# A hybrid convolution and attention kernel on Trainium2: the first attention's pairs of images written out in every engine's program in place of a loop

## What is computed

```python
x = (input - mean) * scale + shift
qkv = einsum('oc,bchw->bohw', pw_w, x)                 # 4 heads of 32 channels
attn = softmax(einsum('bnchw,bncyx->bnhwyx', q, k) / sqrt(32), over the last axis x)
out = einsum('bnhwyx,bncyx->bnchw', attn, v); x = out_w @ out + out_b + input
# then, on the 1024 tokens of each image:
t = t + attention(layernorm(t))     # 64 heads of 2 channels, causal in blocks of 512, rmsnorm on q and k
t = t + experts(layernorm(t))       # 8 experts, three 128x128 products each, gated by a softmax
```

## Time and profile before

| | us |
|---|---|
| median of 3 runs | 3389.75 |
| the three runs | 3385.29 to 3397.03 |
| profiled execution, its own time | 3398.41 |
| profiled execution, span from first to last instruction | 3396.7 |
| PE busy | 3078.5 (91%) |
| ACT busy | 2711.0 (80%) |
| DVE busy | 2062.5 (61%) |
| POOL busy | 263.9 (8%) |

### The profile page before, as it was taken

The page is one execution under the profiler, slowest core; times in us unless marked ns, Lnnn a source line. Parts: engine busy times, 40 slices in busy tenths (PEclk is TensorE's granted clock), DMA queues, the critical chain, the costliest instruction groups (busy, mean ns, idle before and its releaser), DMA issues.

```text
span 3396.7 us, 70341 instructions
## 1 busy us (share of the span) xinstructions
PE 3078.5 (91%) x27633; PEld 1087.3 (32%) x27633; DVE 2062.5 (61%) x2974; ACT 2711.0 (80%) x2580; POOL 263.9 (8%) x350
## 2 busy tenths in 40 slices
PE   6899999999798898998999899899998988999999
PEld 3444444444322222222222222222222222233444
DVE  4788878888656456556556556656656643443333
ACT  5444444445499999999999999999999999973555
POOL 6000000000110011011010110101101000000000
PEclk9899999999899999999999999999999999998999
DMA  6121211120100110210210210210210211001000
GB/s 224 53 53 44 53 47 34 44 52 20 53 16 18 59 26 18 61 27 17 59 29 18 59 27 20 59 27 17 60 29 18 59 27 37 19 15 63 13 12 12
DMA packets 132542, 135.73 MB, mean 40 GB/s; under 512 B 27414, under 2 KB 111476, under 8 KB 132220
## 3 DMA queue, kind: packets, MB, share of 16 engines
q1 hardware_dynamic: 131216, 130.44, 13.9%
q10 hardware_dynamic: 1004, 0.83, 0.1%
HBM read 70.31 MB, written 51.41 MB: 36 GB/s over the span
## 4 chain that ended last, share of the span: by engine, by line
ACT 39%; PE 35%; issue 19%; DVE 5%; DMA 1%; SPq 1%; ACTq 0%; POOL 0%; DVEq 0%
ACT arena L961 38%; PE ps L1318 5%; PE ps L1371 3%; PE ps L1040 3%; PE ps L1365 3%; PE ps L1087 3%; PE ps L1406 3%; PE ps L1114 3%; PE ps L1089 3%; PE ps L1098 2%; PE ps L1069 2%; PE ps L1270 2%; DVE arena L1480 1%; DVE arena L1487 1%; DVE arena L1492 1%
## 5 line engine op out<-in xcount | busy, mean ns | idle before, releaser
L961 ACT ACTIVATE arena<-ps 128x1536 f32<-128x1536 f32 x1536 | 2068.3, 1636 | 21.6 <-PE ps L1270 21.2
L1318 PE MATMUL ps<-arena 128*32 128x512 f32 (+3 forms) x12288 | 1257.8, 504 | 1.9 <-DVE arena L1755 1.7
L1755 DVE TENSOR_TENSOR arena<-arena,causal 128x512 f32<-128x512 f32 x1024 | 664.5, 688 | 314.1 <-ACT arena L961 304.6
L1270 PE MATMUL ps<-arena 15*128 15x512 bf16 (+3 forms) x6144 | 606.9, 331 | 160.7 <-ACT arena L961 151.1
L890 ACT ACTIVATE arena<-ps 128x512 f32<-128x512 f32 x512 | 299.8, 596 | 278.8 <-PE ps L1089 268.2
L1270 PEld LDWEIGHTS ps<-arena 15*128 15x128 bf16 x6144 | 163.0, 92 | 1100.6 <-ACT arena L961 958.7
L1318 PEld LDWEIGHTS ps<-arena 128*32 128x32 f32 x12288 | 284.7, 109 | 385.1 <-issue 331.4
L1480 DVE TENSOR_REDUCE arena<-ps 128x32 bf16<-128x1024 f32 x256 | 311.2, 1216 | 119.9 <-PE ps L1069 119.9
L1487 DVE TENSOR_TENSOR arena<-arena,ps 128x512 f32<-128x512 f32 x512 | 329.2, 680 | 33.5 <-PE ps L1098 32.6
L1740 DVE COPY arena<-ps 128x512 f32<-128x512 f32 x256 | 176.5, 690 | 219.9 <-PE ps L1318 218.9
L1087 PE MATMUL ps<-arena 96*128 96x256 bf16 x1024 | 260.7, 279 | 0.3 <-ACT arena L863 0.2
(11 more groups left out here) (200 smaller groups left out, 1970.9 us busy)
## 6 DMA issues: line engine op xcount, KB each, us to landing
arena<-qstack SPq DMA_DIRECT2D x512, 30.0 KB
parts<-arena SPq DMA_DIRECT2D x8, 1536.0 KB, 6.3
arena<-parts SPq DMA_DIRECT2D x48, 256.0 KB, 5.4
arena<-parts SPq DMA_DIRECT2D x96, 128.0 KB, 2.8
arena<-kstack SPq DMA_DIRECT2D x512, 24.0 KB
qstack<-arena SPq DMA_DIRECT2D x24, 384.0 KB, 3.3
attn<-arena SPq DMA_DIRECT2D x512, 12.0 KB
arena<-arena SPq DMA_DIRECT2D x384, 16.0 KB, 1.8
```

The costliest lines, as they stand in the source:

```text
L961: act.activation(PR1[:, at:at + CW], bank(BPC * (f % 2), BPC), ACT.Exp).then_inc(d_exp, 1)
L1270: mm = pe.matmul(bank(at + k)[:, s * P:(s + n) * P], Ks[par][HR * h:HR * h + QROWS, j * P:(j + 1) * P], Qs[par][HR * h:HR * h + QROWS, t * ...
L1318: mm = pe.matmul(o[HR * h:HR * (h + 1), :], V1[n % 2][:, j, v:v + HR], pr[:, h * HALF + s * P:h * HALF + (s + k) * P], start=not opened[hi ...
L1755: dve.tensor_tensor(v, v, m3, ALU.min).then_inc(d_mask, 1)
```

## The change

The loops over pairs of images become Python loops, so every pair is written out in the program of every engine with `i` as a number. The experts' loops at the end stay.

```diff
-        def peeled(eng, n, body):
-
-            body(0)
-            with eng.Fori(1, n) as i:
-                body(i)
-
         def turns(eng, body, drained):
-            body(0, range(TURN))
-            with eng.Fori(1, B // 2) as i:
+            for i in range(B // 2):
                 body(i, range(TURN))
             for k in range(TAIL + 1):
                 body(B // 2, range(k, k + 1))
...
-            feed(0)
-            with sp.Fori(1, B // 2 - 1) as i:
-                feed(i)
-            feed(B // 2 - 1, last=True)
+            for i in range(B // 2):
+                feed(i, last=i == B // 2 - 1)
...
-            peeled(pool, NSTEP // 2 - 1, pool_b)
+            for i in range(NSTEP // 2 - 1):
+                pool_b(i)
...
-            peeled(pe, B // 2, pe_a)
+            for i in range(B // 2):
+                pe_a(i)
```

## The result

Over 19 runs of each kernel the median went from 3387.88 us to 3378.12, a ratio of 0.9971 with a 95% interval of 0.996 to 0.9982: 9.8 us faster, by the interval between 6 and 14. A second comparison (experiment e6) gave 0.9973, interval 0.9959 to 0.9988. So the sign was right and the time lies in the range, but only a little over half of the expected gain came. A ratio of 0.9971 is just inside "within 0.3%", to which the prediction gave 0.14, against 0.81 for more.

The account below looks back on a forecast made before the run. PE was taken to bound stage B (busy 720.35 of 775 us). Net 16.4 us at four boundaries plus 1.9 from constants, say 18, took the median 3389.75 to 3371.8 us; range 3363 to 3382.

Parts of the forecast that it names:

- the ways back: Stage B, steps 128 and 192, where PE's loop branch waits for instructions: 8.88 and 7.69 us, expected to become 1.5 each.
- the wait for the queries: Stage B image boundaries: PE waits for SP's query loads; without the branch a stop of 1.2 to 2.0 us remains.
- constants in place of registers: Stage B, pairs 1 to 3: 24 groups of eight steps each 0.08 us shorter, 1.9 us saved.
- the mid-pair boundaries: Stage B, steps 96 and 160 in SP's loop: excess of 3.54 and 4.41 us, expected to become 1.5 each.
- step 1 of the sum: Stage B boundaries 96, 128, 160, 192: from 24.52 to 6.0 us, less 2.1 for one clock drop, net 16.4 saved.
- steps 64 and 224: Stage B boundaries fed by written-out SP code: losses of 1.17 and 1.39 us, clock 1.00, taken as the pattern after the change.
- step 2: Stage B, pairs 1 to 3: waits as constants make 24 groups 0.08 us shorter each, 1.9 us saved.
- each stop still drops the clock: Rival, stage B: all four boundaries followed by a low clock of 2.1 us, saving 12, giving 3378; chance 0.17.
- The branch was not what PE waited for: Rival, steps 128 and 192: the stall stays with the queries, only 3 us saved, giving 3386.5; chance 0.05.
- A late fetch: Rival: written-out straight-line code starves once or twice, 4 us each, giving 3376 to 3380; chance 0.05.
- A bad phase: Rival, second attention: 32 more head groups dip from 16.12 to 17.01 us, 11 us slower, giving 3400.6; chance 0.06.

Follow-up runs that it names:

- e6: The changed kernel run again without an edit: 3377.51 us against 3385.2 for the kernel before, ratio 0.9973.
- e2: The changed kernel with PE's loop over pairs kept, everything else written out: 3385.03 us, ratio 0.9992 to the kernel before.
- e5: The kernel before, all loops in place, with SP's six query loads moved ahead of the 12 moves: 3376.91 us against 3385.2, ratio 0.9975.
- e1: The kernel before with only PE's program written out; ACT, DVE, SP and POOL keep their loops: 3379.93 us against 3387.98, ratio 0.9981.
- e9: Repeat of the changed kernel with SP's query loads moved ahead of the 12 moves: 3362.87 us, ratio 0.9923 to the kernel before.
- e3: The changed kernel with SP's six query loads moved ahead of the 12 moves: 3359.89 us, ratio 0.9928 to the kernel before.
- e8: The changed kernel with only SP's loop put back: 3375.1 us against 3385.2 for the kernel before, ratio 0.9973.
- e10: The kernel before with only PE's program written out and SP's query loads moved ahead of the moves: 3364.35 us, ratio 0.9931.
- e4: The kernel before run again without an edit: 3389.08 us, ratio 1.0.

## Why the prediction was right or wrong

**Right: the ways back.** The prediction had them at 8.88 + 7.69 us and left 2 x 1.5, saving 13.6. Over two profiles of before (8.92, 7.75, 6.61, 8.26: mean 7.9) and three of the changed kernel (1.61, 0.64, 1.63, 1.60, 1.43, 0.96: mean 1.3) it is 13.2. That the wait for the queries would take over part of the stall was right as well, and e2 and e5 show the branch as PE's own cost. The figure of about 108 ns that the Trainium skill gives (Advanced Engine Details and Errata, Control Flow Timing) does not hold for a jump back over a pair: it takes 3.4 to 4.6 us here.

**Right: constants in place of registers.** 24 groups of 23.86 us became 23.79: 1.8 us, forecast 1.9. e1 and e2 show that all of it is PE's.

**Wrong: the mid-pair boundaries, in step 1 of the sum.** It took 3.54 and 4.41 us at steps 96 and 160 as what SP's loop costs and expected 1.5 each instead, 5 us saved. Measured, the two boundaries cost 2.8 us in the mean before (3.59, 4.46, 1.47, 1.57) and 2.8 after (1.58, 4.57, 1.25, 1.96, 6.01, 1.56): nothing saved. The excess in the earlier trace rows was two falls of the clock which a second profile of the same program does not have. The prediction saw that 1.96 us of stop had kept the clock and 1.88 had lost it, and drew the right conclusion for the kernel after, where it allowed a fall; it did not draw it for the kernel before, and so compared an execution with four falls with an expectation of one.

**Wrong: steps 64 and 224 counted as safe.** The sum left them at 1.17 and 1.39 us. In the profile after, both lost the clock and cost 4.27 and 3.23. Over three profiles the boundaries 32, 64 and 224 cost 2.1 us in the mean, before 1.6: 1.5 us given back over the three, by chance as far as can be seen. In all eight profiles whose queries come late there are 50 boundaries that are not a way back; the clock fell behind 9 of them, and these cost 4.4 us in the mean where the 41 others cost 1.5, so 2.9 us for a fall. All nine came behind stops of 1.58 to 1.88 us. Eight other stops of that length (1.63 to 1.96 us) kept the clock, and none of the 33 shorter ones lost it. So the length does count in these profiles, though it doesn't decide alone.

**Missing: a fall behind stage B.** Some 15 us after the last step PE waits 2.01 us for DVE, before and after. Windows from there on, the changed kernel first, then the kernel before:

```profile
847.96:852.20 4.24, 4.24 (x10) 1.84 (x11) 0.61 (x1) 0.39 (x1) 0.00 (x0) 0.60 0.07 16
```

```profile
862.44:866.70 4.26, 4.26 (x30) 2.06 (x30) 2.18 (x4) 1.19 (x2) 0.00 (x0) 1.00 0.07 15
```

Same stop, same order of instructions, but PEclk is 0.60 in the first and 1.00 in the second. The counts of 10 and 30 overstate it, since short matmuls come at the end; PE starts its fourteenth matmul behind the stop (L1091, before L1098) 4.61 us after the first one in the changed kernel and 2.93 us after it in the kernel before. From stage B's last step to the first copy of the second attention it takes 96.25, 96.23 and 96.11 us in the three profiles of the changed kernel and 94.38 and 94.57 in the two of before: 1.7 us given back. e1 and e9 have it too (96.21, 96.28); e3, e8 and e10 (94.42, 94.40, 93.38) have not, nor have e2 and e5, whose PE keeps the loop. That makes five of eight profiles with PE written out and none of four with its loop; whether the change brings it or chance does stays open.

**Sum.** Step 1 of the prediction's sum, forecast at 16.4 us, came to 13.2 + 0 - 1.5 = 11.7. With the 1.8 of step 2 and the 1.7 given back behind stage B that makes 11.8 us by five profiles, against 9.8 by the timed runs and 9 by e6's ratio (7.7 by its medians). Stage B itself is 13.6 us shorter in the mean of the profiles (772.2 and 767.0 before, 758.8, 752.9 and 756.2 after). The 2 us between are within what five profiles can tell: the second attention alone takes 2060.95 to 2069.02 us in them, which was the scatter that the prediction named, and the first profile of before was 10.5 us above its median.

Rivals: "each stop still drops the clock" came nearest, with its 3378, but by luck: of its four boundaries one, none and one lost the clock in the three profiles of the changed kernel, and the saving was smaller for another reason, that a second profile of the kernel before has two falls and not four. "The branch was not what PE waited for" is out by e2 and e5. A late fetch of written-out code did not show: outside the boundaries and the falls behind them the groups hold 23.79 us throughout. A bad phase of the second attention did not come systematically: its time is 2067.5, 2066.1 and 2061.0 us against 2069.0 and 2064.2 before.

## What to carry to other kernels

A hardware loop whose body is long costs the engine on the critical path a fetch at each turn, 3.4 to 4.6 us here. Write out that engine's program first: most of the gain was PE's (stage B 756.2 us for PE alone, 752.9 to 758.8 for all; the ratios are 0.9981 and 0.9971, with intervals that overlap). The others' loops count once nothing else stops that engine at the same place: 1.1 and 1.6 us at the two ways back in e10. Look at the same time for what else is late at that point: here one load, queued behind twelve moves on SP though its own condition was met earlier, cost 15 to 18 us at seven boundaries with the clock falls behind them, as much as both ways back (13.2 us) or more, and putting it ahead gives 3360 to 3363 us, which beats both kernels. And before a low clock in one profile is priced as the program's, take a second profile of the same program: of 17 stops of 1.58 to 1.96 us 9 lost the clock, and none of 33 shorter ones.

## What the runs showed of the hardware

- **A jump back was dear over a long body only.** PE's compare-and-branch took 3.4 to 4.6 us over a pair of images (e2, e4, e5), and 0.2 us in stage A and in the experts' loop, whose bodies are short. Lengths between were not tried. The row of the kernel before, ns:

```profile
L1416 PEldq COMPARE_BRANCH  x7: 76/212/226, 3134.2 to 3392.1; - x7
```

  The Trainium skill (Runtime: NRT & Kernel Launch, Instruction fetch mechanics) says that a taken branch whose target is outside the current window of two pages forces a DMA fetch of the target's page before execution goes on. The traces agree on the fetch: a block of 16 KB arrives within each of the eight long branches, 1.3 to 1.5 us before its end (e5). No run shows how many pages the window has. That ACT and DVE show 40 to 63 ns for the branch and stand for 2.2 to 2.6 us behind it (e10) means that the branch's own record is not the place to read the cost on every engine.

- **SP's DMA issues were slower while a block of PE's instructions arrived.** A turn of 12 moves on SP takes 7.5 us or up to 8.9. In the changed kernel, two turns:

```profile
528.97 8.69 SPq L521 DMA_DIRECT2D arena<-arena  x12
...
629.04 7.54 SPq L521 DMA_DIRECT2D arena<-arena  x12
```

  In the first a block arrives for PE, and one of the 12 issues takes 1.5 us in place of 0.6; in the second none does. The instruction queue in the first window:

```profile
q8 instruction: 1, 0.02, 1.0%
```

  Over 240 turns in eight traces (all but the first of stage B and the 31st), the 66 without a block of PE's in them take 7.47 to 7.77 us, mean 7.55, and the 174 with one 7.48 to 8.88, mean 8.25. The queries are queued behind such a turn, so this goes with the stops of 0.56 us at step 192 and 1.88 at 160, which follow the two turns shown. It is a correlation in the traces; no run varied it on purpose.
